# Two sets of part buffers in stage one, loads of unit 0 spread over two batches, and turned copies of q read in order

## The reference, cut to what matters

```python
# x: (4, 1024, 128), 16 heads of 8, rel_key: (256, 8)
def attn(x, Wq, bq, Wk, bk, Wv, bv, Wo, bo, rel_key):
    q, k, v = (split_heads(x @ W + b) for W, b in ((Wq, bq), (Wk, bk), (Wv, bv)))
    scores = einsum('bhid,bhjd->bhij', q, k)
    rel = einsum('bhid,pd->bhip', q, rel_key)
    bias = take_along_axis(rel, clip(j - i + 255, 0, 255), axis=3)
    logits = where(j <= i, (scores + bias) * 8 ** -0.5, -inf)
    return merge_heads(softmax(logits) @ v) @ Wo + bo

def ffn(x, ...):                       # hidden 512, ternary weights, a scale per output
    h = silu(tlin(x, w1, s1)) * tlin(x, w2, s2)
    h = gelu(tlin(h, h1, sh1)); h = gelu(tlin(h, h2, sh2))
    return tlin(h, w3, s3)

x = x + layernorm(attn(layernorm(x), ...))
x = x + layernorm(ffn(layernorm(x), ...))
```

## Time and profile before

| | us |
|---|---|
| median of 3 runs | 740.18 |
| lowest and highest run | 736.39, 741.16 |
| the profiled execution's own time | 739.48 |
| its span, from the first to the last instruction | 737.4 |
| busy: PE, DVE, ACT, POOL | 644.0, 540.2, 572.1, 247.7 |
| granted clock of PE, mean over the span | 0.945 |
| stage one: from the start to the first exponential of stage two | 109.0 |

### The profile page before, as it was taken

The page is one execution under the profiler, slowest core; times in us unless marked ns, Lnnn a source line. Parts: engine busy times, 40 slices in busy tenths (PEclk is TensorE's granted clock), DMA queues, the critical chain, the costliest instruction groups (busy, mean ns, idle before and its releaser), DMA issues.

```text
span 737.4 us, 18944 instructions
## 1 busy us (share of the span) xinstructions
PE 644.0 (87%) x8066; PEld 467.7 (63%) x8066; DVE 540.2 (73%) x923; ACT 572.1 (78%) x660; POOL 247.7 (34%) x175
## 2 busy tenths in 40 slices
PE   4877569999999999999999999978799898998993
PEld 2433336676766766857667667655588687786682
DVE  5894787788687877786878777775677668588546
ACT  2784977988989889889898798786577868677573
POOL 2100180370640913706409128000271441731901
PEclk9988767999999999999999999997999999999997
DMA  7487424152241231521412314050300000000001
GB/s 229 110 224 225 133 63 111 35 132 66 50 114 36 73 94 35 128 70 50 106 46 70 96 34 116 24 166 2 100 1 1 0 1 1 1 29 0 5 25 59
DMA packets 39175, 52.82 MB, mean 72 GB/s; under 512 B 5656, under 2 KB 29640, under 8 KB 36680
## 3 DMA queue, kind: packets, MB, share of 16 engines
q1 hardware_dynamic: 39088, 51.58, 25.6%
HBM read 39.00 MB, written 11.81 MB: 69 GB/s over the span
## 4 chain that ended last, share of the span: by engine, by line
PE 53%; DVE 13%; ACT 12%; issue 5%; POOL 2%; DVEq 0%; ACTq 0%; POOLq 0%
PE p_o L1112 16%; PE p_s L1087 13%; PE p_z L1786 8%; PE p_z L1789 8%; DVE probs L1213 6%; ACT probs L1330 6%; PE p_s L1021 5%; POOL hid_lo L1707 1%; DVE res L1967 1%; ACT hid_hi L1890 1%; ACT o_acc L1339 1%; ACT even_b L1034 1%; ACT odd_b L1034 1%; PE p_o L1124 1%; DVE hid_lo L1991 1%
## 5 line engine op out<-in xcount | busy, mean ns | idle before, releaser
L1087 PE MATMUL p_s<-q_sb,k_sb 96*128 96x128 bf16 (+1 forms) x1600 | 172.1, 250 | 9.9 <-ACT probs L1330 4.7
L1330 ACT ACTIVATE probs<-p_s 128x1024 f32<-128x1024 f32 x160 | 156.7, 1017 | 19.9 <-DVE p_s L1222 10.8
L1112 PE MATMUL p_o<-probs,v_sb 128*32 128x128 f32 (+1 forms) x3200 | 159.9, 331 | 7.5 <-ACT o_acc L1339 4.4
L990 POOL TENSOR_SCALAR_AFFINE_SELECT even_b<-even_b 128x2048 f32<-128x2048 f32 x31 | 75.0, 2420 | 261.3 <-ACT even_b L1034 261.3
L1330 ACT ACTIVATE probs<-probs 128x1024 f32<-128x1024 f32 x128 | 133.5, 1055 | 35.7 <-DVE probs L1213 35.4
L1087 PEld LDWEIGHTS p_s<-q_sb,k_sb 96*128 96x128 bf16 x1600 | 113.8, 100 | 69.5 <-issue 29.5
L1213 DVE TENSOR_TENSOR probs<-p_s,even_b 128x1024 f32<-128x1024 f32 x96 | 114.9, 1219 | 16.6 <-PE p_s L1087 16.6
L1112 PEld LDWEIGHTS p_o<-probs,v_sb 128*32 128x32 f32 x3200 | 84.6, 111 | 41.0 <-issue 14.1
L1786 PE MATMUL p_z<-hid_hi,h_hi 128*128 128x512 f32 x256 | 102.0, 399 | 1.7 <-POOL hid_lo L1707 1.7
L1021 PE MATMUL p_s<-q_rows,rel_w 72*128 72x64 bf16 x2048 | 84.5, 197 | 20.1 <-DVE probs L1213 8.7
L1789 PE MATMUL p_z<-hid_lo,h_hi 128*128 128x512 f32 x256 | 100.9, 394 | 0.0
(11 more groups left out here) (182 smaller groups left out, 844.7 us busy)
## 6 DMA issues: line engine op xcount, KB each, us to landing
k_sb<-k_dram SPq DMA_DIRECT2D x48, 192.0 KB
q_sb<-q_dram SPq DMA_DIRECT2D x16, 576.0 KB
q_rows<-qr_dram SPq DMA_DIRECT2D x42, 192.0 KB
q_dram<-q_parts SPq DMA_DIRECT2D x12, 256.0 KB, 3.1
k_dram<-k_parts SPq DMA_DIRECT2D x12, 256.0 KB, 3.2
qr_dram<-q_turned SPq DMA_DIRECT2D x12, 256.0 KB, 3.4
x_all<-in_L_attn_x_dram SPq DMA_DIRECT2D x4, 512.0 KB, 4.2
every<-in_L_ffn_h_w_dram SPq DMA_DIRECT2D x2, 1024.0 KB, 8.4
```

The costliest lines, as they stand in the source:

```text
L990: nc.gpsimd.affine_select(out=far, in_=near, compare_op=ALU.is_ge, fill=0.0, base=-1 - r, pattern=[[0, QB], [-1, MCH * RCH]], channel_mult ...
L1087: last = nc.tensor.matmul(slot[:, c:c + n * BLK], k_sb[hg][:, h * S + j * BLK:h * S + (j + 1) * BLK], ap(q_sb[hg], at, [[HG * S, KROWS], [ ...
L1112: last = nc.tensor.matmul(p_o[32 * h:32 * h + 32, at:at + blocks * BLK], v_sb[hg][:, j, h * 32:(h + 1) * 32], probs[n % PBUFS][:, h, col * ...
L1330: nc.scalar.activation(to, got, ACT.Exp, scale=SCALE).then_inc(t_exp, 1)
```

## The change

- `q_parts`, `k_parts` and `q_turned` exist twice; batch b uses set b % 2. The first set takes room that was kept free (`stored_room`). `m_parts` of batches 0 and 1 go into the rows of `x_all` that their own batch has used, those of batches 2 and 3 share `m_late`.
- The waits for stores move back by a batch: ACT waits for the stores of batch b-2 instead of b-1, for b >= 2 (helper `stored`). New are a wait for m's stores of batches 0 and 1 ahead of the first `copy_act` of the last batch (whose `even_b` lies over `x_all`), and waits for the stores of batch 2 at the end of stage one on DVE and ACT.
- SP loads `q_rows` and the first half of `k_sb`, `q_sb` ahead of the stores of batch 1, and the second half ahead of the stores of batch 2.
- The turned copy names its elements in the order of the source: it reads 1024 neighbours, and writes them 16 bytes apart. Before, it read 256 bytes apart and wrote neighbours. The number of instructions is the same.
- In `bound`, PE waits for `own` only ahead of the first product that reads it.

```diff
-STORED_ROOM = 5184
+STORED_ROOM = 576
...
+    early_parts = [sb(f"{n}0", [128, PARTS, S], BF16, one) for n in ("q_parts", "k_parts", "q_turned")]
...
+    def m_parts(b):
+
+        if b >= 2:
+            return m_late[:, :, :]
+        return x_all[0:H, b * S:(b + 1) * S].bitcast(BF16).rearrange("h (m s) -> h m s", m=MPARTS)
...
     def turned_view(to, part):
 
-        return to[:, part, :].rearrange("p (r i) -> p r i", i=NB)
+        return to[:, part, :].rearrange("p (r i) -> p i r", i=NB)
+
+    def stored(eng, b, sems):
+
+        for done in sems:
+            eng.wait_ge(done[b % 2], (b // 2 + 1) * (16 * PARTS))
 
     def untouched_view(got, part):
 
-        return got[:, part, :].rearrange("p (i r) -> p r i", i=NB)
+        return got[:, part, :].rearrange("p (i r) -> p i r", i=NB)
...
             if b == 1:
-                for done in (s_qst, s_kst, s_rst):
-                    sp.wait_ge(done, 16 * PARTS)
+                stored(sp, 0, (s_qst, s_kst, s_rst))
                 sp.dma_start(q_rows[:, :], ap(qr_dram, 0, [[DROW, PARTS * HD], [0, PARTS], [1, UH * S]])).then_inc(t_qr[0], 16)
-                for hg in range(2):
-                    load_k(0, hg)
-                    load_q(0, hg)
+            if b in (1, 2):
+                load_k(0, b - 1)
+                load_q(0, b - 1)
...
-            if b > 0 and part == 0:
-                act.wait_ge(s_rst, 16 * PARTS * b)
-            nc.scalar.activation(turned_view(q_turned, part), untouched_view(q_parts, part),
+            if b >= 2 and part == 0:
+                stored(act, b - 2, (s_rst,))
+            nc.scalar.activation(turned_view(q_turned[b % 2], part), untouched_view(q_parts[b % 2], part),
                                  ACT.Identity).then_inc(s_turned, 1)
...
             if last_batch:
+                act.wait_ge(s_mst[0], 16 * 2)
                 for c in range(FIRST_BEFORE):
                     copy_act(act, "even", c)
 
-            if not first:
-                act.wait_ge(s_turned, b * PARTS)
-                act.wait_ge(s_qst, b * (16 * PARTS))
-                act.wait_ge(s_kst, b * (16 * PARTS))
-            nc.scalar.activation(q_parts[:, 0, :], qf[:, :], ACT.Identity).then_inc(s_hi, 1)
+            if b >= 2:
+                act.wait_ge(s_turned, (b - 1) * PARTS)
+                stored(act, b - 2, (s_qst, s_kst))
+            nc.scalar.activation(q_parts[b % 2][:, 0, :], qf[:, :], ACT.Identity).then_inc(s_hi, 1)
...
-            if not first:
-                act.wait_ge(s_mst, b * 16)
+            if last_batch:
+                act.wait_ge(s_mst[1], 16)
...
-            pe.wait_ge(s_own, b + 1)
             for j in range(2):
                 c = slice(j * 512, (j + 1) * 512)
                 nc.tensor.matmul(p_tr[0:2 * GAP, c], k_sel[:, 0, :], q_pos[:, c], start=True, stop=False)
                 nc.tensor.matmul(p_tr[0:2 * GAP, c], k_sel[:, 1, :], qf[:, c], start=False, stop=False)
+                if j == 0:
+                    pe.wait_ge(s_own, b + 1)
                 nc.tensor.matmul(p_tr[0:2 * GAP, c], hneg[:, :], own[:, c], start=False, stop=True).then_inc(s_u, 1)
```

More of the change, by code:

```diff
@@ L249, in build @@
     far_keep, near_cap = (sb(n, [128, MCH * RCH], F32, one) for n in ("far_keep", "near_cap"))
+    early_parts = [sb(f"{n}0", [128, PARTS, S], BF16, one) for n in ("q_parts", "k_parts", "q_turned")]
     sb("stored_room", [128, STORED_ROOM], F32, one)
     exp_warm = sb("exp_warm", [128, 1], F32, one)
-    q_parts, k_parts = (sb(n, [128, PARTS, S], BF16, one) for n in ("q_parts", "k_parts"))
-    m_parts = sb("m_parts", [H, MPARTS, S], BF16, one)
-    q_turned = sb("q_turned", [128, PARTS, S], BF16, one)
+    q_late, k_late = (sb(f"{n}1", [128, PARTS, S], BF16, one) for n in ("q_parts", "k_parts"))
+    m_late = sb("m_late", [H, MPARTS, S], BF16, one)
+    turned_late = sb("q_turned1", [128, PARTS, S], BF16, one)
+    q_parts, k_parts, q_turned = zip(early_parts, (q_late, k_late, turned_late))
+    def m_parts(b):
+        if b >= 2:
+            return m_late[:, :, :]
+        return x_all[0:H, b * S:(b + 1) * S].bitcast(BF16).rearrange("h (m s) -> h m s", m=MPARTS)
     pone = ExitStack()
@@ L284, in build @@
     s_turned = sem("s_turned")
-    s_rst = sem("s_rst")
+    s_rst = [sem(f"s_rst{p}") for p in range(2)]
     s_pos = sem("s_pos")
@@ L295, in build @@
     s_wabs, s_wany = sem("s_wabs"), sem("s_wany")
-    s_qst, s_kst, s_mst = sem("s_qst"), sem("s_kst"), sem("s_mst")
+    s_qst, s_kst, s_mst = ([sem(f"{n}{p}") for p in range(2)] for n in ("s_qst", "s_kst", "s_mst"))
     t_q = [sem(f"t_q{p}") for p in range(2)]
@@ L392, in shift @@
             sp.wait_ge(s_mr, b + 1)
-            sp.dma_start(ap(m_dram, b * (H * S), [[S, H], [DROW, MPARTS], [1, S]]), m_parts[:, :, :]).then_inc(s_mst, 16)
+            sp.dma_start(ap(m_dram, b * (H * S), [[S, H], [DROW, MPARTS], [1, S]]), m_parts(b)).then_inc(s_mst[b // 2], 16)
         def store(b, to, rows, part, got, done):
             sp.dma_start(ap(to, rows[0] * part + b * (H * S), [[S, H], [rows[1], HD], [1, S]]),
-                         got[:, part, :]).then_inc(done, 16)
+                         got[b % 2][:, part, :]).then_inc(done[b % 2], 16)
         def turned(b, part):
@@ L427, in sync_one @@
             turned(B - 1, part)
[L428 to L431, removed]
+        for b in (B - 2, B - 1):
+            stored(sp, b, (s_qst, s_kst, s_rst))
+        for p in range(2):
+            sp.wait_ge(s_mst[p], 16 * 2)
         sp.wait_ge(s_gap, B + 3)
@@ L510, in shift_rest @@
             dve.wait_ge(s_mneg, b * 2 + 2)
-            nc.vector.scalar_tensor_tensor(out=m_parts[:, 1, :], in0=p_tr[0:H, :], scalar=-1.0, in1=m_parts[:, 0, :],
+            nc.vector.scalar_tensor_tensor(out=m_parts(b)[:, 1, :], in0=p_tr[0:H, :], scalar=-1.0, in1=m_parts(b)[:, 0, :],
                                            op0=ALU.mult, op1=ALU.subtract).then_inc(s_mr, 1)
@@ L623, in vector_one @@
         dve.wait_ge(s_low, B * 2)
+        stored(dve, B - 2, (s_qst, s_kst, s_rst))
     def scalar_one(act):
@@ L682, in batch @@
             act.wait_ge(s_rest, b * 2 + 1)
-            nc.scalar.activation(q_parts[:, 1, :], q_rest[:, :], ACT.Identity).then_inc(s_mid, 1)
+            nc.scalar.activation(q_parts[b % 2][:, 1, :], q_rest[:, :], ACT.Identity).then_inc(s_mid, 1)
             act.wait_ge(s_rest, b * 2 + 2)
-            nc.scalar.activation(k_parts[:, 1, :], k_rest[:, :], ACT.Identity).then_inc(s_mid, 1)
+            nc.scalar.activation(k_parts[b % 2][:, 1, :], k_rest[:, :], ACT.Identity).then_inc(s_mid, 1)
             if not last_batch:
@@ L696, in batch @@
                 act.wait_ge(s_u, b * 2 + j + 1)
-                nc.scalar.activation(m_parts[:, 0, j * 512:(j + 1) * 512], p_tr[0:H, j * 512:(j + 1) * 512],
+                nc.scalar.activation(m_parts(b)[:, 0, j * 512:(j + 1) * 512], p_tr[0:H, j * 512:(j + 1) * 512],
                                      ACT.Identity, scale=-1.0).then_inc(s_mneg, 1)
@@ L715, in scalar_one @@
         act.wait_ge(s_vst, B)
+        stored(act, B - 2, (s_qst, s_kst, s_rst))
     def tensor_one(pe):
```

19 lines of the change are left out of this document (9 added, 10 removed).

## The result

| | before | after |
|---|---|---|
| median, lowest to highest of 4 runs each, us | 738.28, 735.77 to 741.16 | 756.03, 755.55 to 756.31 |
| ratio after / before, 95% interval | | 1.0233, 1.0204 to 1.0263 |
| the profiled execution: time, span, us | 739.48, 737.4 | 755.84, 754.1 |
| ScalarE busy, us | 572.1 | 603.5 |
| first exponential of stage two, us | 108.99 | 125.70 |

The change made the kernel slower by 2.3%. In the profiled executions all of it lies in stage one: the first exponential comes 16.7 us later, and so does the end.

What follows compares the result with a forecast made beforehand. Stage two keeps its own pace, so the gain is how much earlier stage one lets its first exponential start: 8.4 + 0.8 = 9.2 us off 739.48 gives 730.3, or 731.0 on the median's scale; range 727.5 to 736.0.

Steps and rivals of the forecast that it cites:

- The turned copy: ScalarE, stage one: reading neighbours and writing 16 bytes apart takes 1.05 us, 0.93 us less for each copy.
- Rival 2: ScalarE's turned copies: the strided write costs more than the read did, 3.8 us a copy; 8.8 us slower, 749; chance 0.06.
- break-even at 3.1: Turned copy's price, some 3.1 us a copy, from which the dearer write decides over the gain in stage one.
- The waits for stores: ScalarE, batch 2: the 8.88 us stall goes, part 0 follows `q_pos` at 63.99, and TensorE's bound is late next.
- rival 1: Turned copy on ScalarE: a strided write costs what the strided read cost, 1.98 us; 6.3 us gained, 733.9; chance 0.26.
- The tail: Batch 3 after `kf`: the old order holds up to 108.96, and TensorE's higher clock gains 0.8 us, between 0 and 1.4.
- The last three copies: Batch 3's turned copies on ScalarE: shortening gains nothing, `low_k` hides them; they cost only if ending 1.5 us later.
- The queue: Loads and stores from 45 us: 8.2 MB at 214 GB/s, until 83; ScalarE's waits for m's stores are in time.
- rival 3: Store queue, stage one: at 180 GB/s or with late issues, m of batch 3 waits 2 to 3 us; 733.5; chance 0.06.
- 8.4 rather than 5.85: Start of `qf` of batch 3: 8.4 us earlier with copies at 1.05 us, 5.85 with copies at 1.98.

Runs made afterwards that it cites:

- the first experiment: The change with the turned copy back in its old order (reads 256 bytes apart, writes neighbours), against the kernel before: 732.97 us, ratio 0.9912.
- the last: The change with the old copy order, plus GpSimd's masks of the last batch waiting until `own` of batch 3 is done: 731.86 us, 0.9907 of the kernel before.

## Why the prediction was wrong, by its own steps

**The turned copy.** This is the step that failed: "I take 1.05". It measured 4.80, four and a half times that, and outside both of the bounds (1.05 and 1.98). Two arguments led there. "Waiting for data belongs to reads rather than to writes" is refuted as a ground for free writes: a 4-byte write 16 bytes apart costs as much as the strided read (2.00), and that of a 2-byte element is the dear one. And the two rows that were to show that "a step by itself is not slow" didn't bear on it: one reads 4 bytes apart, where four elements share 16 bytes, the other reads PSUM. None was a strided write into SBUF, so the upper bound of 1.98 was a guess on symmetry. The new order alone made the whole loss (1.0258), and the change without it gained (0.9912).

**Rival 2** named the mechanism's size and place (a lone 2-byte element that is written costs more, two copies ahead of the root, the last three past `low_k`), and had 0.06. Its price was too low, 3.8 against 4.80, or 4.26 from start to start and 0.3 more in the instruction behind. Its arithmetic was near: at 3.91 it said 8.8 and the first exponential moved 9.65. Its break-even at 3.1 was too high. Between the ratios at 1.89 and 2.96 us (0.9912 and 1.0054) a line crosses 1 at 1.89 + 1.07 x 0.0088 / 0.0142 = 2.55.

**The waits for stores.** Right. With the old copy the stall was gone, part 0 of batch 2 stood at 64.12 (63.99 said), and TensorE's bound was what held `qf` back. `qf` of batch 3 stood at 76.14 in the first experiment and at 77.66 in the last (77.45 said); `p_k`, reckoned at 3.02 us, took 1.88 in the one and 3.07 in the other. The whole was 0.9% as rival 1 had it, but that the first exponential moved by 6.32 where 6.3 was said is luck: `qf` gained 7.16 in place of 5.85, and the tail lost 0.8 where it was to gain 0.4. That either measure would have been enough was not seen: each removes the stall alone.

**The tail.** "DVE and ScalarE wait for `kf`, then everything to 108.96 follows in the old order", 0.8 us gained. In the changed kernel it held without the gain (23.57 us from `kf` to the end of `low_k`, against 23.6). With the old copy the tail grew to 24.4, by `own`: TensorE was faster by the clock, as I reckoned, and thereby let GpSimd in ahead of VectorE. The prediction named instructions that fall otherwise against GpSimd's as a way to be wrong, but its 0.8 counted the faster clock as a gain alone.

**The last three copies.** "Worth nothing", hidden by 1.5 us: no run made them shorter, but with the old copy `low_k` still came last, with 0.35 us of cover. The cost that was named for the case that the cover ends came to 6.1 us.

**The queue and rival 3.** No wait for m's stores appeared in any trace; right.

**8.4 rather than 5.85** for copies at 1.05 was not testable whole. The one part that was tested, a copy of batch 2 taken off ScalarE, brought 1.86 us at `qf` behind the same wait for TensorE, and nothing that the time could show.

**The range** of 727.5 to 736.0 was too narrow, since it rested on 1.98 as the most that a copy could cost. The step from the row of neighbours to that of the strided read is a factor of 1.9; the same factor once more on the unseen write (3.8) was in the rivals, and would have had to be in the range.

## What to carry to other kernels

An access form that no row of the trace shows (here a strided write) has no upper bound by analogy; a probe of a few instructions gives its price, and it should be measured before cost is moved onto it. When a transposing copy of 2-byte elements must stride on one side, let it stride on the read, or write neighbouring pairs where the layout allows it. When a stall is removed, ask how many of the edits are each enough, and what the next engine's bound leaves of the gain. When two runs are compared at one instruction, compare first what the other engines did ahead of it: with TensorE's clock `qf` of batch 3 moved by 1.5 us between two runs with the same program up to there (76.14 and 77.66).

## What the runs showed of the hardware that I had not expected

- A 2-byte element written into SBUF 16 bytes from the last costs 4.6 ns on ScalarE and GpSimd and 2.4 on VectorE, where neighbours cost 1.0, 1.0 and 0.42 (0.43 us for 1024); on ScalarE it costs as much at 256 bytes. Read 256 bytes apart, an element costs 1.9, 1.9 and 1.0 ns.
- A 4-byte write at 16 or 256 bytes costs 1.9 to 2.0 ns on ScalarE, and two 2-byte elements side by side, written 16 bytes apart, 1.1 each.
- An instruction on ScalarE right behind such a 2-byte copy takes 0.3 us longer (1.34 and 1.35 in place of 1.05 to 1.09).
- VectorE's `own` and GpSimd's mask, started 0.1 to 0.3 us apart: the second pays, `own` 2.1 us, or the mask 0.8 (3.20 against 2.38). The Trainium skill, "SBUF — State Buffer", section "Who interferes with whom", says that a VectorE instruction with two SBUF inputs contends with a GpSimd instruction that reads SBUF; the traces agree (`own`, `q_rest`, `k_rest` and `low_k` have two such inputs), and `vo_all`, with one input in PSUM, kept its 1.21 beside a running mask.
